# Moving the clamp of the square sums ahead of the cosine product in a transformer kernel on one NeuronCore

## Chip, cores and metric

One core of a Trainium2 chip runs the kernel. The metric is the device time of one execution in microseconds (us), the median over several runs.

## What is computed

The input is x, 2 sequences x 1024 tokens x 128 channels, float32. A first attention layer (16 heads of 8 channels, a causal window of 32 keys) is added to x with layer norms around it. Then six layers follow, and they take most of the time. Each has a local attention with 16 heads of 64 channels and a gated feed-forward layer:

```
q = l2norm(q) * qs                      # l2norm(t) = t / max(norm(t), 1e-12)
k = l2norm(k) * ksc
q = q * cos * scale + rotate_half(q) * sin * scale
k = k * cos * inv + rotate_half(k) * sin * inv
out = local_attention(q, k, v)          # windows of 32, softmax of 8 * q.k
...
x = attn_layer(shift_tokens(x), ...) + x
x = ffn_layer(shift_tokens(x), ...) + x
```

A clamp at 1e-24 of the sum of squares stands for the maximum with 1e-12 of the norm.

## The kernel before

**Tiles and layers.** The 2048 tokens are 16 tiles of 128 tokens, one token per partition. Six layers run over the 16 tiles. Each engine has a program of its own, written by hand, and the engines meet only at semaphores. Layers 0 and 5 are written out, layers 1 to 4 are a hardware loop; within a layer tiles 0, 1, 14 and 15 are written out, and tiles 2 to 13 are a hardware loop over pairs (`tiles`, L197). In the loops addresses and the values that are waited for lie in registers, so the program has register instructions there (shown as ISA or REGISTER_ALU in the order of instructions).

**One tile body.** The body of tile t finishes the attention of tile t and prepares q, k and v of tile t + 1. Four blocks of 512 columns of q and k are rotated for it, called j = 0 to 3 here (q, k of heads 0 to 7, then q, k of heads 8 to 15). Per rotation Q = 4t + j:

- TensorE projects a block into a PSUM bank (`project`, L1180 to L1182).
- ScalarE squares the bank into `sq` (L494) and signals pj_act.
- VectorE (`rotary`, L783 to L806) waits for pj_act, and for w_ready at Q - 1, since its buffers are used every second rotation. It sums the squares per head into `n2` (L791), multiplies the bank by the cosine table into `tc_` (L794), waits for the sum (n2_ready) and clamps it into `n2c` (L798), and multiplies the halves by the sine table into `ts_` (L801, twice).
- GpSimd (`rotate`, L312) waits for the clamp and raises it to the power -0.5 (`rn`, L317), waits for the sine products and adds `tc_` and `ts_` (`tsum`, L319), and multiplies the two (`w_nat`, L322).
- TensorE transposes `w_nat` (L1187), ScalarE copies the result out (L516).

VectorE's body of a tile (`tile`, L923) is: maxima of the scores of the first eight heads (L748), rotation 0, the output of the second half of tile t - 1 (`heads_out`: reciprocal L756, `o_nat` L758), rotation 1, the residual of tile t - 1 (L765, L766), the copy of the last 32 keys (L773), maxima of the other eight heads, rotation 2, `heads_out` of the first half of tile t, the low part of the input split (`xs_lo`, L780), rotation 3. In the first body of a layer `heads_out` of the tile before and the residual are missing; the last body has no rotations.

ScalarE makes the exponentials (L478), four heads at a time, with the squares and copies between them. TensorE transposes the probabilities (L1153) and `o_nat` (L1193), weighs the values (L1166), projects the output (L1201) and makes the next scores (L1137, L1146). At the end of a layer four groups of four tiles go through the feed-forward layer, and the first rotations of the next layer are started between them.

Of the kernel before, what the change touches and what calls it, by code (L numbers as in the profile page):

```python
# [45 lines left out]
def build(nc, x, Wa, ba, Wp, bp, Wqkv, Wo, scales, W1, W2, par, rope, ident, identb, mask, mask_l, select, out):  # L46
    f32, f32r, bf16 = mybir.dt.float32, mybir.dt.float32r, mybir.dt.bfloat16
    ALU, ACT, AX = mybir.AluOpType, mybir.ActivationFunctionType, mybir.AxisListType
    ctx = ExitStack()
    with ctx:  # L50
        def sb(name, shape, dt=f32):
            return ctx.enter_context(nc.sbuf_tensor(name, shape, dt))

        def sem(name):
            return ctx.enter_context(nc.semaphore(name))
# [55 lines left out]
        n2 = sb("n2", [P, 2, 8])  # L111
        n2c = sb("n2c", [P, 2, 8])
# [53 lines left out]
        n2_ready, n2c_ready = sem("n2_ready"), sem("n2c_ready")  # L166
# [17 lines left out]
        def at_least(eng, s, value):  # L184

            if not (isinstance(value, int) and value <= 0):
                eng.wait_ge(s, value)
# [486 lines left out]
        def _(eng):  # L674
# [108 lines left out]
            def rotary(t, n, j, fresh=False):  # L783

                Q, r, pj = t * 4 + j, j % 2, PJ[QK_AT[j] % 2]
                eng.wait_ge(pj_act, t * 6 + (QK_AT[j] + 1))
                if not (fresh and j < 2):
                    at_least(eng, w_ready, Q - 1)

                heads3 = "p (h d) -> p h d"  # L790
                nc.vector.tensor_reduce(n2[:, r, :], sq[:, r, :].rearrange(heads3, d=D), AX.X, ALU.add  # L791
                                        ).then_inc(n2_ready, 1)
                k = 2 * (j % 2)
                nc.vector.tensor_tensor(  # L794
                    tc_[:, r, :].rearrange(heads3, d=D), pj[:, :].rearrange(heads3, d=D),
                    ropeL[:, k, n, :].rearrange("p (o d) -> p o d", o=1).to_broadcast([P, 8, D]), ALU.mult)
                eng.wait_ge(n2_ready, Q + 1)
                nc.vector.tensor_scalar(n2c[:, r, :], n2[:, r, :], 1e-24, None, ALU.max).then_inc(n2c_ready, 1)  # L798
                for a in range(2):
                    lo, hi = a * (D // 2), (1 - a) * (D // 2)  # L800
                    last = nc.vector.tensor_tensor(  # L801
                        ts_[:, r, :].rearrange(heads3, d=D)[:, :, lo:lo + D // 2],
                        pj[:, :].rearrange(heads3, d=D)[:, :, hi:hi + D // 2],
                        ropeL[:, k + 1, n, lo:lo + D // 2].rearrange("p (o d) -> p o d", o=1
                                                                     ).to_broadcast([P, 8, D // 2]), ALU.mult)
                last.then_inc(pj_dve, 1)  # L806
# [52 lines left out]
            def start(l, part):  # L859

                t0 = l * TILES
                if part == 0:
                    input_rest(t0, 0, 0)
                    input_rest(t0 + 1, 1, 1)
                if part == 1:
                    eng.wait_ge(rope_ready, l * 4 + 4)
                    rotary(t0, 0, 0, True)
                if part == 2:
                    rotary(t0, 0, 1, True)
                if part == 3:  # L870
                    rotary(t0, 0, 2, True)
                if part == 4:
                    copy_prev(t0, 0, 0)
                if part == 5:
                    rotary(t0, 0, 3, True)
# [581 lines left out]
```

## Time and profile before

| | |
|---|---|
| median of three runs | 2511.0 us (2504.93 to 2565.73) |
| the profiled execution | 2513.5 us, its span 2511.7 us |
| mean granted TensorE clock | 0.966 |
| busy in the span: PE, DVE, ACT, POOL | 2084.1, 1743.5, 1632.6, 1740.9 us |

PE is TensorE, DVE is VectorE, ACT is ScalarE, POOL is GpSimd. No engine is busy all the time; the chain of waits passes through all four. The first attention layer takes the first 280 us or so, the six layers run from about 320 us on. The profile names as releaser of a wait the event that came last, also where an instruction waited for several semaphores.

### The profile page before, as it was taken

What the parts mean: (1) busy time and instruction counts of PE and PEld (TensorE: products, weight loads), DVE (VectorE), ACT (ScalarE), POOL (GpSimd) and SP (SyncE); (2) the same over time, 40 slices, a digit from 0 to 9 for tenths busy, and PEclk for the clock granted to TensorE, in tenths of its full rate; (3) what the DMA queues carried; (4) which work ended last, traced back from release to release, by engine and by line L of the source; (5) the groups of instructions that cost most, each with busy time, mean ns of one, the idle gap of its engine ahead of it and who ended that gap; (6) DMA issues with size and microseconds to landing.
All of it is one profiled execution on the core that took longest, in us unless ns stands there. A gap on an engine that the chain in (4) does not pass through costs nothing.

```text
span 2511.7 us, 70965 instructions
## 1 busy us (share of the span) xinstructions
PE 2084.1 (83%) x23552; PEld 1533.5 (61%) x23552; DVE 1743.5 (69%) x4197; ACT 1632.6 (65%) x5654; POOL 1740.9 (69%) x1364
## 2 busy tenths in 40 slices
PE   6999478888888888888888888888788888888886
PEld 4666356666566666466666466665466665566663
DVE  4555667777667777577776777775777776777764
ACT  3555257767567777577776577776577775777772
POOL 4333468888578787588885788885788885888860
PEclk9999779999999999999999999999999999999998
DMA  1000111111021111111111121111211110111110
GB/s 61 1 0 0 43 53 49 40 38 38 22 75 40 46 40 39 53 45 38 38 48 33 54 50 40 38 39 34 63 41 47 39 38 22 48 44 44 38 37 17
DMA packets 40902, 98.65 MB, mean 39 GB/s; under 512 B 6480, under 2 KB 20432, under 8 KB 39856
## 3 DMA queue, kind: packets, MB, share of 16 engines
q1 hardware_dynamic: 40752, 96.75, 14.9%
q8 instruction: 82, 1.34, 0.2%
q14 instruction: 68, 0.56, 0.1%
HBM read 20.32 MB, written 1.05 MB: 9 GB/s over the span
## 4 chain that ended last, share of the span: by engine, by line
PE 39%; issue 19%; DVE 17%; ACT 15%; POOL 8%; DVEq 1%; POOLq 0%; ACTq 0%; DMA 0%; SPq 0%
ACT prob L478 10%; PE bank L1201 5%; PE bank L1146 5%; DVE nmax L748 3%; PE bank L1193 3%; PE bank L1187 3%; DVE ts_ L801 3%; PE bank L1137 3%; DVE o_nat L758 2%; PE bank L1180 2%; ACT qT L516 2%; POOL tsum L319 2%; PE bank L1182 2%; PE bank L1181 2%; PE bank L1050 2%
## 5 line engine op out<-in xcount | busy, mean ns | idle before, releaser
L317 POOL TENSOR_TENSOR rn<-n2c,half_neg 128x8 f32<-128x8 f32 x384 | 632.9, 1648 | 351.0 <-DVE n2c L798 341.8
L478 ACT ACTIVATE prob<-bank,nmax 128x96 f32<-128x96 f32 x1536 | 508.7, 360 | 401.9 <-DVE nmax L748 401.7
L319 POOL TENSOR_TENSOR tsum<-tc_,ts_ 128x512 f32<-128x512 f32 x384 | 493.3, 1285 | 0.0
L1153 PE MATMUL bank<-idf,prob 128*96 128x128 f32 x1536 | 247.2, 285 | 241.6 <-ACT prob L478 241.6
L322 POOL TENSOR_TENSOR w_nat<-tsum,rn 128x512 f32<-128x512 f32 x384 | 401.0, 1044 | 37.8 <-POOL tsum L319 15.1
L791 DVE TENSOR_REDUCE n<-nat 128x8 f32<-128x512 f32 x384 | 261.3, 680 | 188.9 <-ACT nat L494 122.3
L478 ACT ACTIVATION_READ_ACCUMULATOR prob<-bank,nmax 128x1 f32 x1536 | 347.0, 226 | 0.0
L1153 PEld LDWEIGHTS bank<-idf,prob 128*96 128x96 f32 x1536 | 152.9, 128 | 301.1 <-issue 288.6
L1180 PE MATMUL bank<-w_hi,xs 128*128 128x512 f32 x576 | 288.9, 502 | 9.5 <-DVE ts_ L801 7.0
L801 DVE TENSOR_TENSOR ts_<-bank,ropeL 128x256 f32<-128x256 f32 x768 | 285.8, 412 | 0.0
L748 DVE TENSOR_REDUCE nmax<-bank 128x4 f32<-128x384 f32 x384 | 196.1, 552 | 125.5 <-PE bank L1146 117.6
L494 ACT ACTIVATE nat<-bank 128x512 f32<-128x512 f32 x384 | 235.5, 613 | 55.7 <-PE bank L1182 54.0
L794 DVE TENSOR_TENSOR tc_<-bank,ropeL 128x512 f32<-128x512 f32 x384 | 261.2, 680 | 0.0
L780 DVE TENSOR_TENSOR xs_lo<-xA,xs 64x128 fp32r<-64x128 f32 x192 | 189.0, 984 | 72.7 <-ACT xs L427 69.5
L1187 PE MATMUL bank<-idf,w_nat 128*128 128x128 f32 x1536 | 233.5, 275 | 4.2 <-POOL w_nat L322 2.8
L1182 PE MATMUL bank<-w_hi,xs_lo 128*128 128x512 f32 x576 | 232.5, 404 | 0.5 <-issue 0.5
L1181 PE MATMUL bank<-w_lo,xs 128*128 128x512 f32 x576 | 232.9, 404 | 0.0
L1187 PEld LDWEIGHTS bank<-idf,w_nat 128*128 128x128 f32 x1536 | 192.8, 141 | 62.7 <-issue 6.9
L1166 PEld LDWEIGHTS bank<-vspace,pT 96*64 96x64 f32 x6144 | 195.0, 138 | 52.5 <-issue 52.5
L1166 PE MATMUL bank<-vspace,pT 96*64 96x64 f32 x6144 | 221.5, 225 | 0.0
L487 ACT ACTIVATE pT<-bank 96x512 f32<-96x512 f32 x384 | 213.1, 608 | 11.2 <-PE bank L1153 9.0
L1201 PE MATMUL bank<-oT,wo 128*128 128x128 f32 x1536 | 209.1, 280 | 4.1 <-ACT oT L507 4.1
(129 smaller groups left out, 3988.1 us busy)
## 6 DMA issues: line engine op xcount, KB each, us to landing
vspace<-v_nat SPq DMA_DIRECT2D x96, 384.0 KB, 4.0
vspace<-v_nat SPq DMA_DIRECT2D x96, 256.0 KB, 3.5
vspace<-v_nat SPq DMA_DIRECT2D x95, 128.0 KB, 2.3
nat<-w_qkv SPq DMA_DIRECT2D x5, 1536.0 KB, 7.8
wo<-w_o SPq DMA_DIRECT2D x6, 512.0 KB, 4.0
w<-w SPq DMA_DIRECT2D x6, 341.0 KB, 3.0
shared<-w_qkv SPq DMA_DIRECT2D x1, 1536.0 KB, 6.6
w<-w SPq DMA_DIRECT2D x6, 192.0 KB, 3.0
```

The costliest lines, as they stand in the source:

```text
L317: nc.gpsimd.tensor_tensor(rn[:, r, :], n2c[:, r, :], half_neg[:, 0:8], ALU.pow).then_inc(pool_step, 1)
L319: nc.gpsimd.tensor_tensor(tsum[:, r, :], tc_[:, r, :], ts_[:, r, :], ALU.add).then_inc(pool_step, 1)
L322: nc.gpsimd.tensor_tensor(w_nat[:, r, :].rearrange("p (h d) -> p h d", d=D), tsum[:, r, :].rearrange("p (h d) -> p h d", d=D), rn[:, r, :] ...
L478: last = nc.scalar.activation(prob[:, 4 * b + i, :], SB[b][:, i * SPAN:(i + 1) * SPAN], ACT.Exp, bias=nmax[:, p, 8 * G + 4 * b + i:8 * G + ...
L801: last = nc.vector.tensor_tensor(ts_[:, r, :].rearrange(heads3, d=D)[:, :, lo:lo + D // 2], pj[:, :].rearrange(heads3, d=D)[:, :, hi:hi + ...
L1153: last = nc.tensor.transpose(RING[at][0:SPAN, i * P:(i + 1) * P], prob[:, 4 * b + i, :], idf[:, :])
L1166: last = nc.tensor.matmul(OB[qs, a:a + D], pT[:, 4 * b + i, qs], vw[:, p, half, head * D:(head + 1) * D], start=True, stop=True, skip_grou ...
L1180: nc.tensor.matmul(PJ[x % 2][:, :], xs[:, p, :], hi, start=True, stop=False)
L1181: nc.tensor.matmul(PJ[x % 2][:, :], xs[:, p, :], rest, start=False, stop=False)
L1182: nc.tensor.matmul(PJ[x % 2][:, :], xs_lo[:, p, :], hi, start=False, stop=True).then_inc(pj_ready, 1)
L1187: last = nc.tensor.transpose(RING[at][:, i * P:(i + 1) * P], w_nat[:, j % 2, i * P:(i + 1) * P], idf[:, :])
L1201: last = nc.tensor.matmul(YB[:, 0:P], wo[:, 4 * G + i, :], oT[:, G, i * P:(i + 1) * P], start=G == 0 and i == 0, stop=G == 1 and i == 3)
```

## The change

In `rotary` the wait for the sum and the clamp move from behind the product with the cosine table to directly behind the sum. In the changed kernel the clamp is L795 and the product is L796. Nothing else differs, and no instruction is added or taken away.

```diff
                 nc.vector.tensor_reduce(n2[:, r, :], sq[:, r, :].rearrange(heads3, d=D), AX.X, ALU.add
                                         ).then_inc(n2_ready, 1)
                 k = 2 * (j % 2)
+                eng.wait_ge(n2_ready, Q + 1)
+                nc.vector.tensor_scalar(n2c[:, r, :], n2[:, r, :], 1e-24, None, ALU.max).then_inc(n2c_ready, 1)
                 nc.vector.tensor_tensor(
                     tc_[:, r, :].rearrange(heads3, d=D), pj[:, :].rearrange(heads3, d=D),
                     ropeL[:, k, n, :].rearrange("p (o d) -> p o d", o=1).to_broadcast([P, 8, D]), ALU.mult)
-                eng.wait_ge(n2_ready, Q + 1)
-                nc.vector.tensor_scalar(n2c[:, r, :], n2[:, r, :], 1e-24, None, ALU.max).then_inc(n2c_ready, 1)
```

VectorE, in the hardware loop over tiles, rotation 0 (`n` is the sum, a line with - stood before, one with + stands now):

```order
 L187 ISA
 L791 TENSOR_REDUCE n<-nat 128x8
-L794 ISA
-L794 TENSOR_TENSOR tc_<-bank,ropeL 128x512
-L797 REGISTER_ALU
-L798 TENSOR_SCALAR n2c<-n 128x8
+L794 REGISTER_ALU
+L795 TENSOR_SCALAR n2c<-n 128x8
+L796 ISA
+L796 TENSOR_TENSOR tc_<-bank,ropeL 128x512
 L801 ISA
 L801 TENSOR_TENSOR ts_<-bank,ropeL 128x8x32
```

The clamp has moved ahead of the product, and the register instruction of the product's address now stands behind the clamp.

VectorE, in a tile that is written out, rotation 0, before:

```order
L748 TENSOR_REDUCE nmax<-bank 128x4 x2
L791 TENSOR_REDUCE n<-nat 128x8
L794 TENSOR_TENSOR tc_<-bank,ropeL 128x512
L798 TENSOR_SCALAR n2c<-n 128x8
L801 TENSOR_TENSOR ts_<-bank,ropeL 128x8x32 x2
L756 RECIPROCAL linv<-lsum 128x8
L758 TENSOR_TENSOR o_nat<-bank,linv 128x512
```

The same place now:

```order
L748 TENSOR_REDUCE nmax<-bank 128x4 x2
L791 TENSOR_REDUCE n<-nat 128x8
L795 TENSOR_SCALAR n2c<-n 128x8
L796 TENSOR_TENSOR tc_<-bank,ropeL 128x512
L801 TENSOR_TENSOR ts_<-bank,ropeL 128x8x32 x2
L756 RECIPROCAL linv<-lsum 128x8
L758 TENSOR_TENSOR o_nat<-bank,linv 128x512
```

Here the two instructions change places, with no register instruction near them.

VectorE, in the hardware loop, the residual and the key copy behind rotation 1, which the change leaves as they are:

```order
L765 ISA
L765 REGISTER_ALU
L765 TENSOR_TENSOR xB<-bank,xA 128x1
L766 ISA
L766 TENSOR_TENSOR xB<-bank,xA 128x128
L187 ISA
L773 REGISTER_ALU
```

L766 has a register instruction ahead of it, behind L765, which waits. The orders of TensorE, ScalarE, GpSimd and SP are the same before and after.

## Rows read from the trace of the kernel before

**Rows 1.** Costliest groups: out<-in, shapes, count | busy, mean ns | idle before, releaser.

```profile
L317 POOL TENSOR_TENSOR rn<-n2c,half_neg 128x8 f32<-128x8 f32 x384 | 632.9, 1648 | 351.0 <-DVE n2c L798 341.8
...
L319 POOL TENSOR_TENSOR tsum<-tc_,ts_ 128x512 f32<-128x512 f32 x384 | 493.3, 1285 | 0.0
...
L322 POOL TENSOR_TENSOR w_nat<-tsum,rn 128x512 f32<-128x512 f32 x384 | 401.0, 1044 | 37.8 <-POOL tsum L319 15.1
```

**Rows 2.** Table of waits: total us, times, longest us.

```profile
DVE n L791 <- POOL w_nat L322: 63.6, 38, 1.7
...
PE bank L1193 <- DVE o_nat L758: 49.8, 90, 1.1
```

**Rows 3.** Timeline, looped body from 895: start us, us, engine [idle before <-releaser].

```profile
895.43 1.02 DVE L748 TENSOR_REDUCE nmax<-bank 128x4 f32<-128x384 f32 x2 [0.75 <-PE bank L1146]
...
897.08 1.04 POOL L322 TENSOR_TENSOR w_nat<-tsum,rn 128x512 f32<-128x512 f32 x1
...
897.38 0.61 ACT L494 ACTIVATE nat<-bank 128x512 f32<-128x512 f32 x1
...
898.13 0.69 DVE L791 TENSOR_REDUCE n<-nat 128x8 f32<-128x512 f32 x1 [1.68 <-POOL w_nat L322]
...
898.73 0.68 DVE L794 TENSOR_TENSOR tc_<-bank,ropeL 128x512 f32<-128x512 f32 x1
...
899.33 0.16 DVE L798 TENSOR_SCALAR n2c<-n 128x8 f32<-128x8 f32 x1
899.40 0.75 DVE L801 TENSOR_TENSOR ts_<-bank,ropeL 128x256 f32<-128x256 f32 x2
...
900.07 0.19 DVE L756 RECIPROCAL linv<-lsum 128x8 f32<-128x8 f32 x1
...
900.29 0.69 DVE L758 TENSOR_TENSOR o_nat<-bank,linv 128x512 f32<-128x512 f32 x1
...
901.04 0.66 PE L1193 MATMUL bank<-idf,o_nat 128*128 128x128 f32 x4 [0.52 <-DVE o_nat L758]
```

**Rows 4.** Timeline, the same place in a body of the first layer.

```profile
438.46 1.04 POOL L322 TENSOR_TENSOR w_nat<-tsum,rn 128x512 f32<-128x512 f32 x1
...
438.71 0.61 ACT L494 ACTIVATE nat<-bank 128x512 f32<-128x512 f32 x1
...
439.46 0.69 DVE L791 TENSOR_REDUCE n<-nat 128x8 f32<-128x512 f32 x1 [1.60 <-ACT nat L494]
```

**Rows 5.** Timeline, the body of rows 3 further on, to the next square sum.

```profile
904.00 0.16 DVE L765 TENSOR_TENSOR xB<-bank,xA 128x1 f32 x1 [0.84 <-PE bank L1201]
...
904.16 0.29 DVE L766 TENSOR_TENSOR xB<-bank,xA 128x128 f32 x1
904.41 0.35 DVE L773 TENSOR_SCALAR kT<-kT,follows 128x256 f32<-128x256 f32 x1
...
905.04 1.02 DVE L748 TENSOR_REDUCE nmax<-bank 128x4 f32<-128x384 f32 x2 [0.28 <-PE bank L1146]
...
905.25 1.28 POOL L319 TENSOR_TENSOR tsum<-tc_,ts_ 128x512 f32<-128x512 f32 x1
...
917.38 0.69 DVE L791 TENSOR_REDUCE n<-nat 128x8 f32<-128x512 f32 x1 [1.60 <-ACT nat L494]
```

**Rows 6.** Timeline, the residual in a body that is written out.

```profile
1000.45 0.16 DVE L765 TENSOR_TENSOR xB<-bank,xA 128x1 f32<-128x1 f32 x1 [2.20 <-PE bank L1201]
1000.53 0.28 DVE L766 TENSOR_TENSOR xB<-bank,xA 128x128 f32<-128x128 f32 x1
```

**Rows 7.** Timeline, the key copy beside GpSimd's product, second body of the first layer.

```profile
345.88 1.04 POOL L322 TENSOR_TENSOR w_nat<-tsum,rn 128x512 f32<-128x512 f32 x1 [0.16 <-POOL tsum L319]
...
346.33 0.74 DVE L773 TENSOR_SCALAR kT<-kT,follows 128x256 f32<-128x256 f32 x1
```

**Rows 8.** The chain at the first layer's start; timeline at a later layer's start.

```profile
329.53 1.60 POOL rn L317
...
1046.91 0.50 PE L1180 MATMUL bank<-w_hi,xs 128*128 128x512 f32 x1 [0.30 <-DVE ts_ L801]
```

## The prediction

> **What bounds the kernel now.** I read the costly groups of the page first [rows 1]. The reader is to see GpSimd there: each of the 384 rotations gives it a power (1.65 us), a sum (1.29) and a product (1.04), about 4 us, 16 per tile, and it sat idle 351 us ahead of the power, waiting for the clamp. A tile body takes 917.38 - 898.13 = 19.25 us [rows 5], so GpSimd is the busiest vector engine of the layers, and the table of waits [rows 2] even says that VectorE waited 63.6 us, 38 times, for GpSimd's product. Read alone, these two views promise a gain to whoever releases the power sooner.
>
> The timeline of one tile says otherwise [rows 3]. At 898.13 VectorE's square sum (L791) starts, and the profile names the GpSimd product as its releaser because that ended last, at 897.08 + 1.04 = 898.12. But a release that takes 0.01 us would be a strange one, and the code asks for less: the rotation j = 0 of a tile waits for w_ready at Q - 1, which is the product of rotation j = 2 of the tile before, done at least one whole GpSimd rotation, 4 us, earlier. What it really needed was the square of ScalarE (L494), which ended at 897.38 + 0.61 = 897.99, 0.14 us before. One tile shows it plainly [rows 4]: there the product ends at 439.50, after the square sum has already started at 439.46, and the square ended 439.32, again 0.14 before. So GpSimd does not pace the loop. Its results have time: TensorE transposes the product that ends at 898.12 only behind the exponentials' transposes of the next body (transpose_heads(t, 3)).
>
> What does pace it stands in [rows 3], in order: ScalarE's square, VectorE's sum, product with cosine, clamp, the two products with sine, the reciprocal (L756), o_nat (L758), and then TensorE's transpose of o_nat at 901.04, which sat idle 0.52 us for exactly that. The waits [rows 2] count this 90 times: 14 bodies of 16 in each of six layers, 84, and the closing tiles. Behind that transpose TensorE, VectorE's maxima and ScalarE's exponentials follow and lead to the next square. Whatever VectorE does between square and o_nat lies on this loop, once per tile; that is rotation j = 0.
>
> **The change part by part.** It removes nothing and adds no instruction; per rotation the clamp changes places with the cosine product.
>
> Clamp earlier. Before, it ended 899.33 + 0.16 - 898.13 = 1.36 us after the sum's start. Now it waits for the sum (0.69) and a release. The nearest row for a VectorE instruction behind its own engine's semaphore is the reciprocal and o_nat [rows 3]: 900.07 + 0.19 = 900.26, next start 900.29, so 0.03 after the end. The clamp starts at 0.69 + 0.03 = 0.72 and ends at 0.88, and the power starts 0.48 us sooner. Since GpSimd idles before j = 0, its whole row of work moves 0.48 forward. On the path this is worth nothing, by the above, except at the very start of the layers, where GpSimd's first two rotations stand on the chain [rows 8]: -0.5 us, once. The later products stay hidden under the power: they end 2.2 us after the sum's start, the power ends at 0.96 + 1.65 = 2.6. If that cover went, GpSimd would only lose what it gained.
>
> VectorE's stall. Without a wait an instruction starts before the one ahead of it ends: the cosine product starts 0.60 us after a sum of 0.69 [rows 3]. The clamp waits for that sum, so it starts at 0.72 rather than 0.60: +0.12 us. Before the change the same wait was free, for the product of 0.68 us lay between.
>
> A second, smaller stall. Inside the hardware loops the product needs a register instruction (L796 ISA in the order of instructions) that now stands behind a clamp whose wait isn't met. The nearest case is L765, which waits for TensorE, and L766 behind it with such an instruction between: 904.16 - 904.00 = 0.16 [rows 5]. In an unrolled tile the same pair has none, and takes 1000.53 - 1000.45 = 0.08 [rows 6]. Before the change the sine product followed the clamp by 0.07 [rows 3]. I read this as the queue running ahead only while waits are met. So sum to sine products was 1.27 and becomes 0.72 + 0.16 + 0.60 = 1.48, +0.21 us, in looped tiles, and 0.72 + 0.07 + 0.60 = 1.39, +0.12 us, in unrolled ones. Bounds: nothing at all, if the clamp is issued like an instruction without a wait; above, the dearest gap behind a wait that these rows show, 0.16, in both places: 0.69 + 0.16 - 0.60 = 0.25, plus 0.09, so +0.34. I take the two nearest rows, since each is the same engine in the same kind of place.
>
> The Trainium skill has a rule against this cost: VectorE: DVE Perf Modes, section The DRAIN you can't avoid, says that the next operation waits for the pipe anyway and that a semaphore behind each one costs nothing extra. By that rule the change would leave VectorE's time where it was, and the sum would be that of the third rival below. Rows 3 disagree: the next start is 0.09 us before the end without a wait, 0.03 after it with one.
>
> The other rotations. j = 1 is followed by a residual that waits 0.84 us for TensorE [rows 5], which covers 0.1 to 0.2. j = 2 is followed by o_nat of the other half, which TensorE reads only behind the probabilities of that half; j = 3 by the maxima, for which VectorE waits 0.75 us [rows 3]. If a cover were gone it would cost that same 0.12 to 0.21. In j = 1 and 2 the clamp is held until GpSimd's running operation ends, as before: the two engines share a way into memory [rows 5, 7]: the copy L773 at 346.33 takes 0.74 instead of 0.35, and ends 0.15 after GpSimd's product. GpSimd is 0.48 earlier, so those clamps end about 0.48 earlier too, and the cosine product behind them is late by no more than 0.12. SP's queue and all DMAs keep their places.
>
> The sum: 72 looped bodies (12 of 16, six layers) x 0.21 = 15.1; 12 unrolled ones x 0.12 = 1.4; at five layer starts TensorE waits for the sine products of j = 1, behind those of j = 0 [rows 8], two unrolled rotations, 5 x 0.24 = 1.2; the start -0.5. Together +17 us. The profiled execution took 2513.5, so 2530.5. The median shown is 2511.0, 2.5 lower; on that footing 2528, which is my number: 0.7% slower. About 2% (50 us) is what a measurement of this kernel can surely tell from no change, so this is no change by that measure.
>
> **Rivals.** 1. Clearly slower: the copy of the last keys (L773) falls into GpSimd's sum. In [rows 5] it starts 904.41 - 898.13 = 6.28 after the square sum, and GpSimd's second sum at 905.25, 7.12 after. The gap of 0.84 shrinks from both sides: GpSimd 0.48 earlier (6.64), the copy 0.21 later (6.49). 0.15 us is left. If it closes, which needs VectorE 0.36 late instead of 0.21, the copy is held until 6.64 + 1.28 = 7.92, ends 0.15 later at 8.07, and the maxima behind it, due at 6.91 + 0.21 = 7.12, come 0.9 late, on the loop. In all 84 bodies: 76 + 17 = +93, 2604; in every second one, +55, 2566. For it: the gap is small. Against: whoever starts first seems to keep the way free, and the copy starts first. The Trainium skill says the same (SBUF — State Buffer, section SBUF: two separate sides: the pair is locked for a whole instruction by whichever starts first); rows 7 agree as far as a late VectorE operation goes.
> 2. The table of waits is right and GpSimd paces 38 tiles: 38 x 0.48 = -18, which cancels the +17: 2511. Against: [rows 4].
> 3. The wait costs nothing and the register instruction hides: -0.5, 2510. Against: rows 3 and 5.
> A real gain over 2% would need 50 us; even 0.48 us in every one of 84 bodies gives 40, so I see no mechanism for it.
>
> **How the numbers follow.** Forecast 0.70, first rival 0.12 (about half of it in every second tile only), second 0.06, third 0.09, something not seen 0.03. The range goes from the second and third rivals' place, 2509, to every second tile's collision, 2565; the first rival's full price is left out. The stall's own bounds (nothing to 84 x 0.34 = 29) give 2511 to 2540 on the median's footing, inside it. Faster by over 2%: 0.02. Within: 0.87. Slower: 0.11.
>
> **What would show it.** In the changed kernel's timeline: the clamp 0.72 after the sum's start; the cosine product 0.16 behind it in looped tiles and 0.07 in unrolled ones; the power 0.48 earlier; L773 still 0.35 us long; a tile body of 19.5 instead of 19.3 us. GpSimd's idle time before the power moves but does not shrink much. I am wrong if tile bodies keep or lose time, if L773 is over 0.6 us in most tiles, or if the sine products end under 0.05 or over 0.35 us later against the square sum.

## The result, and the profile after

| | before | after |
|---|---|---|
| median | 2509.2 us (2504.93 to 2565.73, 4 runs) | 2540.0 us (2533.42 to 2553.49, 4 runs) |
| profiled execution, its span | 2513.5, 2511.7 us | 2553.5, 2551.7 us |
| granted TensorE clock in it | 0.966 | 0.961 |

The ratio is 1.013, with a 95% interval of 1.0085 to 1.0176: slower by 31 us, where 17 were forecast. The profiled execution of the changed kernel is the slowest of its four, 14 us above their median, so what is counted in it may be more than a usual execution holds. Medians here and below leave out nothing, ratios leave disturbed executions out; the profiled executions of two experiments (the wait alone, the early copy) were disturbed ones with whole stretches at a lower clock, so their rows serve for single bodies and only loosely for counts, and of filler B alone in experiment 6 the two undisturbed times of four are given.

Two of the costly groups of the changed kernel (columns as in [rows 1]):

```profile
L317 POOL TENSOR_TENSOR rn<-n2c,half_neg 128x8 f32<-128x8 f32 x384 | 636.1, 1657 | 389.8 <-DVE n2c L795 381.4
...
L791 DVE TENSOR_REDUCE n<-nat 128x8 f32<-128x512 f32 x384 | 261.3, 680 | 202.9 <-ACT nat L494 202.3
```

Its table of waits, and behind it one line of that of the kernel before: total us, times, longest us.

```profile
POOL rn L317 <- DVE n2c L795: 381.4, 206, 13.3
...
DVE n L791 <- ACT nat L494: 202.3, 183, 4.1
...
PEld bank L1193 <- DVE o_nat L758: 76.1, 80, 1.0
PE bank L1193 <- ACT pT L487: 46.5, 66, 0.7
...
PE bank L1193 <- DVE o_nat L758: 18.6, 24, 1.1
```

```profile
PEld bank L1193 <- DVE o_nat L758: 61.3, 80, 0.8
```

GpSimd waits longer for the clamp, not shorter (389.8 us against 351.0, [rows 1]), though each clamp comes sooner: what paces the loop has become slower and GpSimd with it. The 38 waits of the square sum for GpSimd's product [rows 2] are gone, and their time stands under ScalarE's square: they were only its name. Ahead of the transpose of `o_nat` (L1193) TensorE's matmuls wait 46.5 + 18.6 = 65.1 us, where it was 49.8 [rows 2], and its weight loads 76.1, where it was 61.3. VectorE's busy time fell by as much as the kernel got slower, from 1743.5 to 1712.6 us: the low part of the input split (L780) takes 736 ns on average instead of 984 and the clamp 239 instead of 316, and neither made a body quicker. Less busy time on an engine is no gain where another chain sets the pace.

The timeline of one looped body of the changed kernel, to the next square sum:

```profile
902.05 0.69 DVE L791 TENSOR_REDUCE n<-nat 128x8 f32<-128x512 f32 x1 [1.68 <-ACT nat L494]
...
902.77 0.17 DVE L795 TENSOR_SCALAR n2c<-n 128x8 f32<-128x8 f32 x1
...
902.92 0.69 DVE L796 TENSOR_TENSOR tc_<-bank,ropeL 128x512 f32<-128x512 f32 x1
903.03 1.65 POOL L317 TENSOR_TENSOR rn<-n2c,half_neg 128x8 f32<-128x8 f32 x1 [1.93 <-DVE n2c L795]
...
903.52 0.74 DVE L801 TENSOR_TENSOR ts_<-bank,ropeL 128x256 f32<-128x256 f32 x2
903.83 0.61 PE L1153 MATMUL bank<-idf,prob 128*96 128x128 f32 x4 [0.86 <-ACT prob L478]
...
905.16 1.11 PE L1193 MATMUL bank<-idf,o_nat 128*128 128x128 f32 x4 [0.71 <-ACT pT L487]
...
909.70 0.16 DVE L765 TENSOR_TENSOR xB<-bank,xA 128x1 f32 x1 [2.50 <-PE bank L1201]
...
910.04 1.04 POOL L322 TENSOR_TENSOR w_nat<-tsum,rn 128x512 f32<-128x512 f32 x1
910.11 1.12 DVE L773 TENSOR_SCALAR kT<-kT,follows 128x256 f32<-128x256 f32 x1
911.15 1.01 DVE L748 TENSOR_REDUCE nmax<-bank 128x4 f32<-128x384 f32 x2
...
915.54 1.06 PE L1153 MATMUL bank<-idf,prob 128*96 128x128 f32 x4 [1.65 <-ACT prob L478]
...
925.01 0.69 DVE L791 TENSOR_REDUCE n<-nat 128x8 f32<-128x512 f32 x1 [1.60 <-ACT nat L494]
```

Up to 904.19 this is the body that was predicted: clamp at +0.72, product 0.15 behind it, sine products at +1.47 (1.27 before), power at +0.98 (1.44). Then comes what was not. The transposes at L1193 take 1.11 us instead of 0.66, and the residual waits 2.50 us for TensorE instead of 0.84 [rows 5]. The granted clock shows why, by stretches of this body. Behind it stand the same two first stretches of a quick body of the changed kernel (863) and of the kernel before (898). Columns: stretch, length, busy time of PE, PEld (TensorE's weight loads), DVE, ACT and POOL with counts, PEclk (the granted clock as a share of the full one), DMA share, GB/s.

```profile
902.00:905.10 3.10, 1.59 (x22) 1.04 (x18) 2.98 (x8) 3.10 (x12) 2.07 (x2) 1.00 0.19 42
905.10:908.50 3.40, 3.34 (x13) 2.95 (x14) 2.06 (x6) 1.26 (x4) 3.24 (x3) 0.51 0.00 0
908.50:915.40 6.90, 5.09 (x85) 3.94 (x84) 5.28 (x12) 4.21 (x20) 4.86 (x5) 0.99 0.00 0
915.40:918.80 3.40, 3.26 (x12) 2.86 (x13) 1.58 (x3) 2.25 (x5) 1.56 (x2) 0.50 0.00 0
```

```profile
863.07:866.17 3.10, 1.53 (x20) 0.99 (x16) 3.02 (x8) 3.07 (x12) 2.11 (x2) 1.00 0.19 42
866.17:869.57 3.40, 3.38 (x37) 2.76 (x41) 2.44 (x8) 1.68 (x3) 3.24 (x3) 1.00 0.00 0
```

```profile
898.10:901.20 3.10, 1.73 (x23) 1.19 (x20) 3.04 (x8) 3.09 (x12) 1.65 (x3) 1.00 0.19 42
901.20:904.60 3.40, 3.40 (x45) 2.78 (x48) 2.56 (x8) 1.69 (x3) 3.24 (x4) 1.00 0.00 0
```

TensorE runs 3.4 us at half its clock (1.2 of 2.4 GHz) behind the waits of 0.86 us ahead of L1153 and 0.71 us ahead of L1193, and another 3.4 us behind the 1.65 us wait ahead of the last L1153. The quick body at 863 keeps its full clock though TensorE was no busier in its first stretch (1.53 us against 1.59). So what stands here does not yet say which body is struck. In between, the copy of the keys (L773) starts 0.07 us after GpSimd's product and is held to 0.15 us behind its end: 1.12 us instead of 0.35. The body takes 22.96 us.

So I counted bodies: the distance from one square sum of rotation 0 to the next in the trace, for the 66 bodies that follow one another in the hardware loops. A body is either quick or contains such a half-clock stretch (the "slow bodies" of the expectations). The offset is that of the stretch from the square sum.

| profile of | quick body, us | half-clock bodies | their length, us | offsets, us |
|---|---|---|---|---|
| before | 19.29 | 3 | 20.9 | 11.4 |
| after | 19.50 | 11 | 23.0 | 3.1 to 3.6, and again 13.3 to 13.8 |

The 40 us between the two profiled executions are in these numbers: 66 x 0.20 = 13 in all bodies, and half-clock bodies 11 x 3.5 = 39 instead of 3 x 1.6 = 5, so 34; together 47. Outside these bodies the changed kernel was some 7 us faster, at the layers' starts and ends; there its trace has 15 half-clock stretches, that of the kernel before 19. The median execution is 31 us slower, not 40.

TensorE's wait ahead of L1193 is 0.51 to 0.52 us in all 66 bodies of the kernel before and 0.69 to 0.71 us in all 66 of the changed one, quick or not. If the wait matters, it is not by being longer in the bodies that are struck.

### The profile page after: what moved, and what is told of

The parts are those of the page before. It is cut to its first block, busy times and chain, and to the rows that moved or that the text cites. A ratio compares the mean times of both kernels' runs of the same rounds, so it can differ in the third digit from the quotient of the medians.

```text
span 2551.7 us, 70965 instructions
## 1 busy us (share of the span) xinstructions
PE 2099.6 (82%) x23552; PEld 1550.3 (61%) x23552; DVE 1712.6 (67%) x4197; ACT 1634.2 (64%) x5654; POOL 1741.3 (68%) x1364
## 4 chain that ended last, share of the span: by engine, by line
PE 45%; ACT 25%; issue 13%; DVE 11%; POOL 5%; ACTq 0%; DVEq 0%; POOLq 0%; DMA 0%; SPq 0%
ACT prob L478 15%; PE bank L1201 6%; PE bank L1146 6%; DVE nmax L748 4%; PE bank L1193 4%; PE bank L1187 3%; ACT qT L516 3%; ACT nat L494 3%; PE bank L1137 3%; PE bank L1180 3%; PE bank L1182 3%; PE bank L1181 3%; PE bank L1153 3%; ACT pT L487 3%; PE bank L1050 2%
## 5 line engine op out<-in xcount | busy, mean ns | idle before, releaser
L317 POOL TENSOR_TENSOR rn<-n2c,half_neg 128x8 f32<-128x8 f32 x384 | 636.1, 1657 | 389.8 <-DVE n2c L795 381.4
L1153 PE MATMUL bank<-idf,prob 128*96 128x128 f32 x1536 | 247.9, 285 | 248.0 <-ACT prob L478 248.0
L1153 PEld LDWEIGHTS bank<-idf,prob 128*96 128x96 f32 x1536 | 153.5, 128 | 307.7 <-issue 296.0
L494 ACT ACTIVATE nat<-bank 128x512 f32<-128x512 f32 x384 | 235.6, 613 | 63.1 <-PE bank L1182 61.3
L796 DVE TENSOR_TENSOR tc_<-bank,ropeL 128x512 f32<-128x512 f32 x384 | 262.1, 683 | 0.0
L1201 PEld LDWEIGHTS bank<-oT,wo 128*128 128x128 f32 x1536 | 195.0, 199 | 6.5 <-ACT oT L507 6.0
```

What stands on the lines that cost most here:

```text
L317: nc.gpsimd.tensor_tensor(rn[:, r, :], n2c[:, r, :], half_neg[:, 0:8], ALU.pow).then_inc(pool_step, 1)
L494: nc.scalar.activation(sq[:, j % 2, :], PJ[QK_AT[j] % 2][:, :], ACT.Square).then_inc(pj_act, 1)
L1153: last = nc.tensor.transpose(RING[at][0:SPAN, i * P:(i + 1) * P], prob[:, 4 * b + i, :], idf[:, :])
L1201: last = nc.tensor.matmul(YB[:, 0:P], wo[:, 4 * G + i, :], oT[:, G, i * P:(i + 1) * P], start=G == 0 and i == 0, stop=G == 1 and i == 3)
```

## The experiments

All are judged by the ratio to the kernel before, run on the same chip. The diffs are against the changed kernel unless said.

**1. Rotation 0 as before, the others changed.**

```diff
-                eng.wait_ge(n2_ready, Q + 1)
-                nc.vector.tensor_scalar(n2c...)
+                if j:
+                    eng.wait_ge(n2_ready, Q + 1)
+                    nc.vector.tensor_scalar(n2c...)
                 nc.vector.tensor_tensor(tc_...)
+                if not j:
+                    eng.wait_ge(n2_ready, Q + 1)
+                    nc.vector.tensor_scalar(n2c...)
```

> Rotation j = 0 has the clamp behind the cosine product again, rotations 1 to 3 keep the new place. Theory (the loss is VectorE's stall in rotation 0, the only one on the loop): undisturbed looped bodies last 19.29 us as before the change, not 19.49, and the time is that of the kernel before, 2505 to 2515; the power of rotation 0 starts at its old place, so GpSimd's second sum is about 7.1 us behind the square sum again, the key copy is not held in slow bodies, and these last about 20.9 us instead of 23.0. Rival (GpSimd's being early, in any rotation, disturbs VectorE): bodies stay above 19.4 and the time above 2525.

Measured: 2510.4 us, ratio 1.0012 (1.0001 to 1.0023), quick bodies 19.29, 4 half-clock bodies. Three early clamps of four cost nothing to speak of. All of the loss hangs on rotation 0. The early clamps do bring GpSimd's power forward in rotation 3, from 1.44 to 0.97 us behind its sum; in rotations 1 and 2 GpSimd is still at its own work, and the power starts where it did.

**2. Rotation 0 changed, the others as before** (the same diff with the conditions exchanged).

> Only rotation 0 has the clamp early, rotations 1 to 3 stand as before. My theory (the whole loss is rotation 0's): quick bodies 19.48 to 19.50, slow bodies as with the whole change, 2532 to 2545 us. Rival (the early clamps of rotations 1 to 3, by GpSimd's earlier start, make the copy collide and so the bodies of 23 us): those bodies are gone, slow ones take 21 us, time 2520 to 2528.

Measured: 2536.0 us, 1.0109 (1.0089 to 1.0129), quick bodies 19.50. As with the whole change, but 10 half-clock bodies, of which only 2 took 23 us: five had one stretch at 3.1 to 3.6 and no second, three one at 11.5 to 11.7. So the rival has a share in it. The timeline of one body with a stretch right behind L1193 (its square sum stood at 896.27):

```profile
900.43 0.94 DVE L802 TENSOR_SCALAR n2c<-n 128x8 f32<-128x8 f32 x1
...
904.35 0.35 DVE L773 TENSOR_SCALAR kT<-kT,follows 128x256 f32<-128x256 f32 x1
904.41 1.20 POOL L322 TENSOR_TENSOR w_nat<-tsum,rn 128x512 f32<-128x512 f32 x1
```

Here rotation 1's clamp still comes late and GpSimd with it, the copy starts 0.06 us ahead of the product, and now the product is the one that is held (1.20 for 1.04). The early clamps of the other rotations make it lose that race.

**3. The wait alone: the product waits for the sum, the clamp stays behind it.**

```diff
                 eng.wait_ge(n2_ready, Q + 1)
-                nc.vector.tensor_scalar(n2c...)
                 nc.vector.tensor_tensor(tc_...)
+                eng.wait_ge(n2_ready, Q + 1)
+                nc.vector.tensor_scalar(n2c...)
```

> The order of before, with one wait more: the cosine product waits for the sum. The clamp stays behind it, so GpSimd gets nothing early (its power starts 0.12 us later) and the register instruction of the product's address stands ahead of the wait. Theory: the cosine product starts 0.72 us behind the sum's start instead of 0.60, bodies last 19.29 + 0.12 = 19.41 us, 84 of them are 10 us, about +0.4%, and the gap between key copy and GpSimd's second sum stays 0.8 us, so slow bodies last about 21.0. Rival (a wait for a finished or nearly finished operation of one's own costs nothing, and the loss comes from GpSimd being early): 19.29 us, time unchanged.

Measured: 2549.7 us, 1.0165 (1.0147 to 1.0184), quick bodies 19.55, 15 half-clock bodies of 21.1. That is more than expected (19.41, and 10 us in all), and at least as much as the whole change, whose interval it overlaps. The timeline of a looped body:

```profile
901.01 0.69 DVE L791 TENSOR_REDUCE n<-nat 128x8 f32<-128x512 f32 x1 [1.59 <-ACT nat L494]
901.85 0.69 DVE L795 TENSOR_TENSOR tc_<-bank,ropeL 128x512 f32<-128x512 f32 x1 [0.16 <-DVE n L791]
902.46 0.16 DVE L799 TENSOR_SCALAR n2c<-n 128x8 f32<-128x8 f32 x1
```

The product starts 0.84 us after the sum, not 0.72. In the loop it has a register instruction ahead of it, and now the wait stands on that one: it runs only when the sum is done, and adds its 0.12 us. The same trace has the control: rotations 2 and 3 have no register instruction there, and their product starts 0.71 and 0.72 us after the sum, in the median body. The wait, not the clamp, is what costs.

**4. No register instruction for the product** (every tile gets the cosine factors of tile 0, so the kernel leaves out those of the tile's own positions).

```diff
-                    ropeL[:, k, n, :].rearrange("p (o d) -> p o d", o=1)
+                    ropeL[:, k, 0, :].rearrange("p (o d) -> p o d", o=1)
```

> The changed kernel with the cosine product reading the table of tile 0 for every tile, so its output has the wrong cosine factors; the address is then constant and no register instruction stands between clamp and product in the hardware loop. Theory (0.12 us of the stall is the wait, 0.09 the register instruction behind an unmet wait): the product starts 0.07 to 0.08 us behind the clamp's start instead of 0.16, and undisturbed looped bodies last about 19.40 us instead of 19.49. Rival (the register instruction costs nothing, the rest has another source): product still 0.16 behind, bodies 19.49.

Measured: 2526.5 us, 1.0073 (1.0055 to 1.0091), quick bodies 19.42, 5 half-clock bodies. The timeline:

```profile
819.43 0.69 DVE L791 TENSOR_REDUCE n<-nat 128x8 f32<-128x512 f32 x1 [1.68 <-ACT nat L494]
820.15 0.17 DVE L795 TENSOR_SCALAR n2c<-n 128x8 f32<-128x8 f32 x1
820.23 0.68 DVE L796 TENSOR_TENSOR tc_<-bank,ropeL 128x512 f32<-128x512 f32 x1
```

The product stands 0.08 behind the clamp instead of 0.15 (0.13 in the median body). So the 0.20 us of a body are 0.13 for the wait and 0.07 for the register instruction behind it. The register instructions themselves are in the traces: before, that of the product's address ran at 898.15, while the sum of 898.13 was still under way. In the changed kernel it ran at 902.79, 0.01 us after the clamp's start at 902.77, although the sum had begun at 902.05. It waited with the clamp.

**5. The key copy ahead of the residual**, so that it runs while VectorE waits for TensorE, and the same edit on the kernel before as its control.

```diff
+                    if not closing:
+                        copy_prev(t + 1, n + 1, 1 - p)
...
-                    else:
-                        copy_prev(t + 1, n + 1, 1 - p)
```

> The changed kernel with the key copy ahead of the residual instead of behind it, so that it runs while VectorE waits for TensorE. Theory (the part of the loss above 84 x 0.2 us comes from slow bodies, in which TensorE's clock is halved, the copy is late, falls into GpSimd's second sum and is held about 0.75 us, and a second stretch at half clock follows): undisturbed bodies still 19.49, but no body of 23 us any more, slow ones 21.0 to 21.5, copy 0.35 us long nearly everywhere, time 2520 to 2528. Rival (slow bodies are long because of the clock alone): bodies of 23 us remain, and the time stays 2535 to 2545.

> The kernel before with the key copy ahead of the residual, the control for the same edit on the changed kernel, which gained 7 us. My theory (that gain came of copies that were held up in slow bodies): here, where one kind of slow body, without a held copy, is left, nothing is gained: quick bodies 19.29, time 2506 to 2512 us. Rival (the copy's place gains by itself, in each body): quick bodies 19.2 or less, 2500 to 2505 us.

Measured: on the changed kernel 2532.9 us, 1.010 (1.0079 to 1.0122); on the kernel before 2507.7, 0.9991 (0.9975 to 1.0008), quick bodies 19.29, 5 half-clock bodies of 20.9. The bodies of 23 us are gone from the changed kernel, but 11 half-clock bodies of 21.0 to 21.1 stay, 8 of them with the stretch at 11.5. In the other three the copy is still held (0.84 to 1.26 us). The time falls between what I and the rival expected, 7 us under that of the changed kernel, and the two intervals overlap, so that this gain is not shown. The held copy is not the root.

What it costs in a body the traces do tell. With a stretch at 3.1 to 3.6 and nothing else a body takes 20.97 us (experiment 2), with the held copy besides 21.42 (B alone, below): 0.45 us. The second stretch came in all 14 bodies of the changed kernel and experiments 2 and 4 in which the copy was held, and in none of the five of experiment 2 in which it was not. In this experiment and in the wait alone, where the copy was held up in three and in nine bodies, none followed, so the hold alone does not bring it.

**6. Does TensorE's idle time bring the half clock?** Transposes of the identity that nothing reads, written to a bank that the next step overwrites, were put into TensorE's waits: three ahead of L1193 (A) and eight ahead of the last L1153 of a body (B).

```diff
+                        for i in range(3):
+                            nc.tensor.transpose(RING[6][:, i * P:(i + 1) * P], idf[:, :], idf[:, :])
                         transpose_out(t - 1, 1, 6)
...
+                        for i in range(8):
+                            nc.tensor.transpose(RING[6][:, i % 4 * P:(i % 4 + 1) * P], idf[:, :], idf[:, :])
                     transpose_probs(t, 1, 1, 6)
```

A alone on the changed kernel:

> The changed kernel, with three transposes of the identity on TensorE (nothing reads what they write) in the wait ahead of L1193. My theory (the extra slow bodies come of TensorE's granted clock that falls to half behind the idle time ahead of L1193, which grew from 0.51 to 0.70 us): the slow bodies whose half-clock stretch begins 3.1 to 3.7 us behind the square sum, 11 of 66, are 0 to 2, and those with the stretch at 11.5, behind the 1.49 us of idle time ahead of L1153, stay at 3 or 4 as before; body 19.50, time 2515 to 2525 us. Rival (the half clock comes of how busy the whole body is, or starts from another gap): 8 or more slow bodies stay, time 2535 to 2545; a second rival is that the fillers hold up L1193, with quick bodies above 19.6 us.

Both on the kernel before, and both on the changed one:

> The kernel before with the three transposes ahead of L1193 and eight ahead of the last group of L1153, in the wait of 1.49 us. My theory: no slow body is left in the loops (3 before, 1.6 us each), quick bodies stay at 19.29, time 2500 to 2507 us. Rival (the fillers take TensorE past the moment at which the exponentials are ready): quick bodies of 19.4 us or more, time 2515 us or more.

> The changed kernel with both sets of filler transposes, those ahead of L1193 and those ahead of the last L1153. My theory (the change costs 0.20 us per body, 17 us in all, and what it costs above that is slow bodies): no slow body in the loops, none with a held copy, quick bodies 19.48 to 19.50 us, time 2519 to 2526 us, 16 us above the kernel before with the same fillers (2506). Rival (some of the loss lies elsewhere, in layer starts or in bodies that are held up without a half clock): 2530 us or more.

B alone on the changed kernel:

> The changed kernel with the eight transposes ahead of the last L1153 alone; the wait ahead of L1193 stays as the change made it. My theory (two waits of TensorE, each with a half-clock stretch behind it: the one at 3.1 to 3.6 us behind the square sum and the one at 11 to 14): the slow bodies of 23 us are gone, since their second stretch stood behind the filled wait; those with the stretch at 3.1 stay, some 11 of 66, now at 21 to 21.5 us; none has a stretch at 11.5; time 2524 to 2534 us. Rival (the second stretch comes of the held copy, not of TensorE's wait): bodies of 23 us stay, 2538 us or more. A second rival (what decides is how busy TensorE is over the whole body): no slow bodies at all, 2519.

| kernel | time, us | ratio | quick body | half-clock bodies and offsets |
|---|---|---|---|---|
| before, A and B | 2506.3 | 0.9995 (0.9973 to 1.0017) | 19.28 | 0 |
| after, A | 2530.3 | 1.0062 (1.0032 to 1.0091) | 19.49 | 6 of 21.07, all at 11.5 to 11.7 |
| after, A and B | 2519.4 | 1.0041 (1.003 to 1.0052) | 19.47 | 0 |
| after, B | 2562.8 and 2571.1 | no interval | 19.50 | 22 of 21.4, all at 3.1 to 3.6 |

The timeline of a body of the changed kernel with both (L1314 is the filler A), and behind it the granted clock of its first stretches, columns as above:

```profile
835.17 0.69 DVE L791 TENSOR_REDUCE n<-nat 128x8 f32<-128x512 f32 x1 [1.60 <-ACT nat L494]
...
837.80 0.55 PE L1314 MATMUL bank<-idf 128*128 128x128 f32 x3 [0.23 <-ACT pT L487]
...
838.27 0.66 PE L1193 MATMUL bank<-idf,o_nat 128*128 128x128 f32 x4
...
841.54 0.35 DVE L773 TENSOR_SCALAR kT<-kT,follows 128x256 f32<-128x256 f32 x1
841.81 1.28 POOL L319 TENSOR_TENSOR tsum<-tc_,ts_ 128x512 f32<-128x512 f32 x1
```

```profile
835.10:838.20 3.10, 2.09 (x29) 1.45 (x25) 2.96 (x8) 3.10 (x12) 2.06 (x2) 1.00 0.19 42
838.20:841.60 3.40, 3.40 (x35) 2.72 (x37) 2.54 (x9) 1.71 (x4) 3.24 (x3) 1.00 0.00 0
```

Each filler takes away the stretches behind its own wait and leaves some behind the other. With the filler TensorE waits 0.23 us ahead of it and none ahead of L1193, where it was 0.71, the clock behind L1193 stays full, and with A alone none of the stretches at 3.1 to 3.6 is left. The time with A alone is above what I expected (2515 to 2525), with 6 late stretches where 3 or 4 were said. With both, the change costs what its stalls cost: 66 x (19.49 - 19.31, the mean bodies) = 12 us, and the ratios differ by 0.0046, 11.5 us (5 to 18, estimated from the two intervals). With B alone my expectation was missed by 29 us or more: the 23 us bodies went, as expected, but every second body in long rows became a half-clock one. The starts of the stretches then lie 41 us apart (824.9, 865.8), and 21.4 + 19.5 = 40.9 is two bodies. Why the rhythm locks at this length and how many stretches other lengths get I did not settle.

Side by side the profiles say how far the wait ahead of L1193 goes as a cause. Counted are the stretches at 3.1 to 3.6 us, in one profile each:

| wait ahead of L1193, us | profiles | stretches in 66 bodies |
|---|---|---|
| 0.52 | before, its early copy, experiments 1 and 7 | 0, 0, 0, 0 |
| 0.64 | fixed address | 1 |
| 0.70 | after, first alone, early copy, B alone | 11, 7, 3, 22 |
| 0.78 | wait alone | 9 |
| filled | after with A, both kernels with A and B, experiment 7 with A and B | 0, 0, 0, 0 |

Without the lengthened wait there is no such stretch. How many come with it depends on something else as well, since 3 and 22 stand at the same wait; this stays open.

**7. The clamp behind the sine products**, with no fillers, and with A and B.

```diff
-                eng.wait_ge(n2_ready, Q + 1)
-                nc.vector.tensor_scalar(n2c...)
...
                     last = nc.vector.tensor_tensor(ts_...)
+                eng.wait_ge(n2_ready, Q + 1)
+                nc.vector.tensor_scalar(n2c...)
```

> The clamp stands behind both sine products, ahead of the reciprocal, in all rotations. My theory (what stands between the sum and o_nat on VectorE is on the loop, and nothing else of this chain is): the sine products start at 1.20 us behind the sum's start and not at 1.27, the clamp follows at about 1.95, the o_nat product is no later than before, and a quick body takes 19.22 to 19.30 us (19.29 in the kernel before); time 2503 to 2510 us. Rival (GpSimd's power is near the loop after all, and its start 0.6 to 0.7 us later in each rotation is felt): some rotation waits for w_ready or the transposes, a body of 19.5 to 20 us, time 2530 us or more.

> The clamp behind the sine products and both sets of filler transposes: the version that should beat both kernels if the two theories hold. Theory: quick bodies 19.22 to 19.30 us, no slow ones, time 2494 to 2505 us. Rival: the sum of the rivals of the two parts, 2520 us or more.

Measured: 2511.3 us, 1.0001 (0.9985 to 1.0017), quick bodies 19.28, 6 half-clock bodies of 20.9, all with the stretch at 11.4 to 11.5; with fillers 2504.4, 0.9982 (0.9969 to 0.9995), no half-clock body. The timeline without fillers:

```profile
814.10 0.69 DVE L791 TENSOR_REDUCE n<-nat 128x8 f32<-128x512 f32 x1 [1.68 <-ACT nat L494]
...
815.97 0.16 DVE L806 TENSOR_SCALAR n2c<-n 128x8 f32<-128x8 f32 x1
816.04 0.19 DVE L756 RECIPROCAL linv<-lsum 128x8 f32<-128x8 f32 x1
816.21 1.65 POOL L317 TENSOR_TENSOR rn<-n2c,half_neg 128x8 f32<-128x8 f32 x1 [1.87 <-DVE n2c L806]
816.26 0.69 DVE L758 TENSOR_TENSOR o_nat<-bank,linv 128x512 f32<-128x512 f32 x1
```

GpSimd starts 2.11 us after the sum instead of 1.44, and nothing is late. But `o_nat` stands at +2.16, as before: the clamp's 0.07 us were moved from ahead of the sine products to ahead of the reciprocal, still on the loop, so of the hoped 0.07 nothing came. The version with fillers is the only one that beats the kernel before beyond its interval, by 0.2%. Against the kernel before with fillers (0.9995) the clamp's place is not shown to matter.

## Why the prediction was right and where it fell short

Direction and size class were right: slower, by less than 2%, and 2540 lies in the range. The size was 17 us where the measured one is 31, and that 2540 lies well inside the range is owed to the first rival, which had drawn it up to 2565 and explains little of the 31: the stall's own bounds end at 2540. That part is luck. By its own steps:

- **GpSimd does not pace the loop** ([rows 3, 4]). Held. Its power 0.47 us earlier in rotation 3 (experiment 1), or 0.64 to 0.66 us later in all four (7), changes no quick body; rival 2 falls. The waits table moved 63.6 us to ScalarE's square without VectorE waiting less.
- **Only rotation 0 is on the loop.** Held: the loss is there with rotation 0 alone and gone without it.
- **Clamp at 0.72, +0.12.** Measured 0.72; the wait's part of a body 0.13 (experiment 4). Rival 3 and the Trainium skill's rule (VectorE: DVE Perf Modes, The DRAIN you can't avoid, that a semaphore behind each operation costs nothing extra) fall: the wait alone lengthens a quick body by 0.26 us, and made the kernel 1.65% slower. The rule supposes that the next operation starts only when the pipe is empty; here the instruction without a wait starts 0.09 us before the end of the one ahead.
- **The register instruction, +0.09.** Measured 0.07; product 0.13 behind the clamp in the median body, 0.15 in the one shown, where 0.16 was said. The instruction's own start, at 902.79 with the clamp (experiment 4), shows the reason given, that it doesn't run ahead of an unmet wait.
- **The sum, +17.** Without half-clock bodies the change costs about 12 us (5 to 18), so 17 is neither confirmed nor refuted as a sum. Its terms fare better. The looped body grows by 0.20 us (0.21 said), which makes 14 for 72 of them, and the written-out one ahead of the loop from 19.32 to 19.45, 0.13 (0.12 said). The 1.2 for layer starts can't be told: the first bodies of a layer differ by 1 us and more from layer to layer in one trace.
- **The step that was missing** is one the sum took for granted: that a body which grows by 0.2 us grows by nothing else. The kernel before already had 3 half-clock bodies in its trace, and [rows 3] show the 0.52 us wait ahead of L1193; it became 0.71. The lengthened wait is the price's second half: 2540 - 2519 = 21 us of the 31 go with both fillers (10 with A alone, which is the one in the lengthened wait), which on the kernel before change nothing clear of noise (ratio 0.9995, at most 7 us by its interval). To size it I would have had to read the granted clock by stretches of one body, not as a mean.
- **Rival 1, the copy held by GpSimd.** In quick bodies it did not come: the copy starts 6.38 us after the square sum in the median (6.49 said), GpSimd's sum at 6.63 (6.64 said), and the one that starts first, the copy, takes its 0.35. The Trainium skill's rule (SBUF — State Buffer, SBUF: two separate sides) that the one which starts first keeps the pair of ports agrees with both cases, this one and the held copy at 910.11. In the half-clock bodies the collision came after all, with GpSimd's product instead of its sum, and costs 0.45 us there besides the half clock, 11 x 0.45 = 5 us in the profiled execution. The mechanism was named and its trigger was not.

## What to carry to other kernels

A wait on the engine's own last result is not free because the data are nearly there: it ends the overlap of neighbours (0.12 us here) and holds back the register instructions behind it (0.07 more), so keep an independent instruction between producer and consumer, and release an engine sooner only if it is waited for. The waits table names the last event, which need not be the cause. Where TensorE waits in every tile, read the granted clock of single stretches before and after: a few tenths of a microsecond more idle time can cost more through the clock than by themselves, and a few transposes that nobody reads can buy it back, if they fill every such wait. In the kernel before, with 3 such bodies, they bought nothing that could be measured.

## What the runs showed that I had not expected

The half-clock stretches were 3.4 us long each and cost 1.6 us of a body; they came behind waits of 0.86 and 0.71 us close together, though TensorE was busy 82% of the span and sat idle for 1.65 us at most in such a body. In the changed kernel's trace 11 of 66 bodies had them, all doubled, behind L1193, in the kernel before 3, none there. The other 55 had the same waits and a full clock. Filling only the other wait, of 1.5 us and more ahead of the last L1153, made their number rise to 22, and the kernel took 2563 and 2571 us, 23 and 31 us more than the median with no filler at all.
